# Keys and values from split fp32r operands, and part of a LayerNorm moved to GpSimd, in a gated cross-attention and expert layer

## The reference, cut to what matters

```python
xn = layernorm(x)
q = xn @ Wq + bq;  k = ctx @ Wk + bk;  v = ctx @ Wv + bv          # per head
attn = softmax(q k^T / 4);  a = attn @ v
x1 = x + tanh(g_xattn) * (concat(a) @ Wo + bo)
S  = sigmoid(layernorm(x1) @ Wg)                                  # routing
for each expert e:                                                # 896 tokens with the largest S
    h = gelu(layernorm(x1)[I_e] @ W1_e + b1_e)
    out[I_e] += tanh(g_ffn) * (h @ W2_e + b2_e) * S_e
```

## Time and profile before

| | |
|---|---|
| time, three runs | 893.86, 895.79 (median), 897.25 us |
| the profiled execution | 894.2 us, its span 892.4 us |
| PE busy over the span | 814.0 us (91%) |
| DVE busy | 708.3 us (79%) |
| ACT busy | 571.2 us (64%) |
| POOL busy | 286.0 us (32%) |
| mean granted TensorE clock | 0.961 of full |

### The profile page before, as it was taken

One profiled execution on the slowest core, in us unless ns is written; L12 is line 12 of the kernel. 1 busy time (PEld: TensorE's weight loads), 2 busy tenths in 40 slices (PEclk: granted clock), 3 DMA queues, 4 the chain that ended last, 5 costly groups with the idle time before them and its releaser, 6 DMA issues. The chain is left out here.

```text
span 892.4 us, 22315 instructions
## 1 busy us (share of the span) xinstructions
PE 814.0 (91%) x8336; PEld 667.8 (75%) x8336; DVE 708.3 (79%) x1900; ACT 571.2 (64%) x1251; POOL 286.0 (32%) x269
## 2 busy tenths in 40 slices
PE   5989999999999999999996118999999999999995
PEld 3555888888888888888775006989898988888885
DVE  6888999999999999999875784787676767764542
ACT  2655877787777777877664214847576675849470
POOL 4760111011111111110100603366465655644504
PEclk9999999999999999999998557999999999999998
DMA  7843666776676676666610304162525344453303
GB/s 190 196 93 89 153 157 153 169 180 155 151 184 152 157 165 165 173 154 150 160 33 29 106 1 134 44 153 50 135 54 136 58 130 102 97 131 67 38 6 41
DMA packets 96210, 104.62 MB, mean 117 GB/s; under 512 B 11744, under 2 KB 92272, under 8 KB 96112
## 3 DMA queue, kind: packets, MB, share of 16 engines
q1 hardware_dynamic: 84128, 88.50, 38.5%
q0 software_dynamic: 10752, 14.69, 9.6%
q10 hardware_dynamic: 1232, 0.12, 0.1%
HBM read 39.60 MB, written 14.68 MB: 61 GB/s over the span
## 5 line engine op out<-in xcount | busy, mean ns | idle before, releaser
L485 DVE TENSOR_REDUCE a_nm<-a_pS 112x1 f32<-112x375 f32 x342 | 177.3, 538 | 4.7 <-PE a_pS L791 4.1
L1772 PE MATMUL e_p<-w2hl,e_hh 128*128 128x512 f32 x440 | 156.9, 397 | 0.0
L725 POOL TENSOR_TENSOR a_kp<-a_k_rest,a_kp 128x375 bf16<-128x375 f32 x56 | 50.4, 900 | 323.7 <-ACT a_kp L326 323.7
L785 PEld LDWEIGHTS a_pT<-a_qst,a_kst 98*128 98x128 bf16 x1536 | 102.8, 99 | 40.8 <-issue 11.7
L785 PE MATMUL a_pT<-a_qst,a_kst 98*128 98x112 bf16 x1536 | 123.5, 212 | 1.7 <-ACT a_P L306 1.0
L1566 POOL DMA_INDIRECT out_dram<-e_y,e_idx x56 | 89.1, 1591 | 109.2 <-ACT e_y L1605 103.2
L1774 PE MATMUL e_p<-w2hl,e_hl 128*128 128x256 f32 x440 | 122.8, 279 | 0.0
L1652 DVE TENSOR_TENSOR e_hl<-e_hid,e_hh 128x384 fp32r<-128x384 f32 (+1 forms) x128 | 77.8, 623 | 47.3 <-ACT e_hh L1598 46.3
L306 ACT ACTIVATE a_room<-a_pT 128x448 f32<-128x448 f32 x192 | 96.7, 543 | 28.1 <-PE a_pT L785 27.8
L791 PE MATMUL a_pS<-a_kst,a_qst 96*112 96x375 bf16 x342 | 107.8, 334 | 3.4 <-DVE a_nm L485 3.0
L306 ACT ACTIVATE a_P<-a_pT 128x448 f32<-128x448 f32 x192 | 97.7, 546 | 9.4 <-PE a_pT L785 8.1
(11 more groups left out here) (247 smaller groups left out, 1688.9 us busy)
## 6 DMA issues: line engine op xcount, KB each, us to landing
a_kst<-a_kp SPq DMA_DIRECT2D x192, 192.0 KB, 3.6
w<-in_L_ffn_W_dram SPq DMA_DIRECT2D x16, 1024.0 KB, 6.8
a_qst<-a_qp SPq DMA_DIRECT2D x96, 112.0 KB, 3.0
a_craw<-in_ctx_dram SPq DMA_DIRECT2D x32, 128.0 KB
a_room<-in_x_dram SPq DMA_DIRECT2D x8, 448.0 KB, 6.6
a_xb<-in_x_dram SPq DMA_DIRECT2D x32, 112.0 KB, 3.4
out_dram<-a_x SPq DMA_DIRECT2D x32, 112.0 KB, 2.2
xn_scratch<-a_x SPq DMA_DIRECT2D x32, 112.0 KB, 2.2
```

The source lines that it names most:

```text
L485: dve.tensor_reduce(nm[:, h:h + 1], s_bank(b, h)[0:LQ, 0:LK], AXX, ALU.max, negate=True).then_inc(s_used, 1)
L785: last = pe.matmul(pT[u % 2][:, j * LQ:(j + 1) * LQ], kst[b % 4][:, h, c * 128:(c + 1) * 128], q_of(b, slice(None), h), start=True, stop=True)
L1772: pe.matmul(p2[g % 2][:], hh[:, f, rows], T.w2hl[r % 2][:, f].rearrange("p q d -> p (q d)"), start=(f == 0), stop=(f == 7), skip_group_che ...
```

## The change

1. **Keys and values.** From batch 5 on (`EARLY_C`), cT, wk and wv are split into a high fp32r part and an fp32r rest. Each fp32 matmul becomes three fp32r matmuls into the same bank (high x high, high x low, low x high), padded from 375 to 376 columns. The split of the weights (once) and of cT (`context_high`, `context_low`, once a batch) is done on POOL.
2. **x1 and its LayerNorm.** wo and bo are multiplied by tanh(g_xattn) once on POOL. bo is added to the reloaded x on POOL (`x_biased`), so that `added` alone makes x1 on DVE; `gated` is gone. DVE keeps the statistics and the mean and variance. POOL does the root (`pow` with -0.5, then two Newton rounds) and the scaling to x2 (`x2_of`).
3. **Places.** k_rest, O, cc[0], ccT, x1, x2 and x2T lie in tiles of the prologue that are free by then.
4. **Order.** `weighted(m)` comes near the start of step m instead of `weighted(m+1)` at the end of it; each exponential into a P buffer waits for the `weighted` quarter that read it. PE's, ACT's and DVE's lists are in a new order, and SP's: the row maxima and the queries go ahead of two thirds of the key DMAs, and `x_again(m+2)` takes the place of `x_again(m)`.

```diff
+        tail, xn_flat = room[:, 24 * LQ:], xnT[:].rearrange("p k n -> p (k n)")
+        k_rest = [tail[:, t * LK:(t + 1) * LK] for t in range(2)]
+        cTh, cTl = ([sb(f"cT{p}{i}", [128, LK2], F32R) for i in range(4)] for p in "hl")
...
@@ SP, main loop @@
                 if live(m + 4, 3):
                     stack_keys(m + 4, (0, 1))
-                    stack_keys(m + 4, (2, 3))
-                if live(m):
-                    x_again(m)
-                if live(m + 4, 3):
-                    stack_keys(m + 4, (4, 5))
                 if live(m + 2, 1):
                     row_max(m + 2)
                 if live(m + 5, 4):
                     stack_queries((m + 5) // 2, (3, 4, 5) if (m + 5) % 2 else (0, 1, 2))
+                if live(m + 4, 3):
+                    stack_keys(m + 4, (2, 3))
+                    stack_keys(m + 4, (4, 5))
+                if live(m + 2):
+                    x_again(m + 2)
@@ ACT @@
+                if c == 0:
+                    wait(act, o_ready, 4 * b + quad - 3)
                 act.activation(P[quad][:, c, :], pT[u % 2][:, 0:4 * LQ], ACT.Exp).then_inc(exp_done, 1)
@@ DVE @@
+                dve.wait_ge(xb_ready, b + 1)
                 dve.wait_ge(wo_ready, b + 1)
-                dve.tensor_tensor(xo[:], pM[0][0:LQ, 0:D], bo[:], ALU.add).then_inc(wo_read, 1)
-            def gated(b):
...
-                dve.scalar_tensor_tensor(xo[:], xo[:], gx[0:LQ], xb[p][:], ALU.mult, ALU.add).then_inc(x1_ready, 1)
+                dve.tensor_tensor(xo[:], pM[0][0:LQ, 0:D], xb[p][:], ALU.add).then_inc(x1_ready, 1)
@@ POOL @@
+            def x_biased(b):
+                pool.wait_ge(xb_loaded[b % 2], 16 * (b // 2 + 1))
+                pool.tensor_tensor(xb[b % 2][:], xb[b % 2][:], bo[:], ALU.add).then_inc(xb_ready, 1)
+            def root(b):
+                pool.wait_ge(mv_ready, b + 1)
+                pool.tensor_scalar(ve[:], mv[b % 2][:, 1:2], EPS, None, ALU.add).then_inc(root_set, 1)
+                pool.tensor_scalar(nvh[:], mv[b % 2][:, 1:2], EPS, -0.5, ALU.add, ALU.mult).then_inc(root_set, 1)
+                pool.tensor_tensor(y[:], ve[:], mhalf[:], ALU.pow).then_inc(root_set, 1)
+                for k in range(2):
+                    pool.tensor_scalar(yy[:], y[:], y[:], nvh[:], ALU.mult, ALU.mult).then_inc(root_set, 1)
+                    pool.tensor_scalar(y[:], yy[:], 1.5, y[:], ALU.add, ALU.mult).then_inc(root_set, 1)
+            def x2_of(b):
+                pool.tensor_scalar(x2[b % 2][:], x1[b % 2][:], mv[b % 2][:, 0:1], y[:], ALU.subtract, ALU.mult)\
+                    .then_inc(x2_ready, 1)
+            def context_high(b):
+                pool.wait_ge(ct_copied, b + 1)
+                pool.tensor_copy(cTh[b % 4][:, 0:LK], cT[b % 4][:]).then_inc(ct_high, 1)
+            def context_low(b):
+                pool.tensor_tensor(cTl[b % 4][:, 0:LK], cT[b % 4][:], cTh[b % 4][:, 0:LK].bitcast(F32), ALU.subtract).then_inc(ct_split, 1)
             for m in range(FIRST, LAST):
                 if live(m + 5, EARLY_K):
                     k_low_part(m + 5, 0)
+                if live(m + 6, EARLY_C):
+                    context_low(m + 6)
+                if live(m):
+                    root(m)
+                if live(m + 5, EARLY_K):
                     k_low_part(m + 5, 1)
+                if live(m):
+                    x2_of(m)
+                if live(m + 2):
+                    x_biased(m + 2)
+                if live(m + 7, EARLY_C):
+                    context_high(m + 7)
@@ PE @@
-                pe.matmul(k_bank(b, t)[:, 0:LK], wk[:, t, :], cT[b % 4][:], start=True, stop=True).then_inc(k_ready[t], 1)
+                pe.wait_ge(ct_split, b - EARLY_C + 1)
+                pe.matmul(out, wkh[:, t, :], cTh[b % 4][:], start=True, stop=False)
+                pe.matmul(out, wkh[:, t, :], cTl[b % 4][:], start=False, stop=False)
+                pe.matmul(out, wkl[:, t, :], cTh[b % 4][:], start=False, stop=True).then_inc(k_ready[t], 1)
...
+                    pe.matmul(out, cTh[b % 4][:, k0:k0 + n], wvh[:], start=True, stop=False)
+                    pe.matmul(out, cTh[b % 4][:, k0:k0 + n], wvl[:], start=False, stop=False)
+                    last = pe.matmul(out, cTl[b % 4][:, k0:k0 + n], wvh[:], start=False, stop=True)
```

More of the change, by code:

```diff
@@ new lines, in _ @@
+            pool.wait_ge(scaled, 3)
+            pool.wait_ge(wk_ready, 1)
+            pool.wait_ge(wq_ready, 2)
+            pool.wait_ge(wv_loaded, 16)
+            for t in range(2):
+                pool.wait_ge(q_ready[t], 3 * G)
+            for t in cTh + cTl:
+                pool.memset(t[:, LK:LK2].bitcast(F32), 0.0).then_inc(pads_zero, 1)
+            pool.tensor_copy(wkh[:], wk[:]).then_inc(w_high, 1)
+            pool.tensor_copy(wvh[:], wv[:]).then_inc(w_high, 1)
+            pool.wait_ge(w_high, 2)
@@ L958, in _ @@
                 if live(m + 2, 1):
+                    scores_s(m + 2, 10)
+                if live(m + 1):
+                    scores_t(m + 1, 1)
+                if live(m):
+                    bank_free(m, C_PIECES, "weighted")
+                    weighted(m, 0)
+                    weighted(m, 1)
+                    weighted(m, 2)
+                    weighted(m, 3)
+                if live(m + 2, 1):
+                    scores_s(m + 2, 11)
+                if live(m + 1):
+                    scores_t(m + 1, 2)
+                if live(m + 2, 1):
                     scores_s(m + 2, 12)
                 if live(m + 1):
-                    scores_t(m + 1, 1)
+                    scores_t(m + 1, 3)
                 if live(m + 2, 1):
                     scores_s(m + 2, 13)
+                if live(m):
+                    o_transposes(m, m)
+                if live(m + 1):
+                    scores_t(m + 1, 4)
+                if live(m + 2, 1):
+                    scores_s(m + 2, 14)
                 if live(m - 2):
@@ L966, in _ @@
                 if live(m + 1):
-                    scores_t(m + 1, 2)
+                    scores_t(m + 1, 5)
                 if live(m + 2, 1):
-                    scores_s(m + 2, 14)
+                    scores_s(m + 2, 15)
                 if live(m + 5, EARLY_K):
@@ L972, in _ @@
                 if live(m + 1):
-                    scores_t(m + 1, 3)
-                if live(m + 2, 1):
-                    scores_s(m + 2, 15)
-                if live(m + 1):
-                    scores_t(m + 1, 4)
+                    scores_t(m + 1, 6)
                 if live(m + 3, 2):
@@ L981, in _ @@
                     scores_s(m + 3, 0)
-                if live(m):
-                    o_transposes(m, m)
                 if live(m + 2, 1):
@@ L986, in _ @@
                     values(m + 2, 0)
-                if live(m + 1):
-                    scores_t(m + 1, 5)
-                    scores_t(m + 1, 6)
                 if live(m + 3, 2):
                     scores_s(m + 3, 1)
-                    scores_s(m + 3, 2)
                 if live(m + 2, 1):
@@ L995, in _ @@
                     values(m + 2, 1)
+                if live(m + 1):
+                    scores_t(m + 1, 7)
+                    scores_t(m + 1, 8)
+                if live(m + 3, 2):
+                    scores_s(m + 3, 2)
                 if live(m + 5, EARLY_K):
                     keys_at_once(m, m + 5, 1)
-                if live(m + 1):
-                    scores_t(m + 1, 7)
                 if live(m + 3, 2):
@@ L1019, in _ @@
                     ct_transposes(m + 6)
+                if live(m - 1):
+                    x2_transposes(m, m - 1)
+                if live(m + 1):
+                    scores_t(m + 1, 10)
+                if live(m + 3, 2):
+                    scores_s(m + 3, 6)
+                if live(m + 1):
+                    scores_t(m + 1, 11)
                 if live(m + 3, 2):
                     scores_s(m + 3, 7)
-                if live(m + 3, 1):
-                    scores_s(m + 3, 8)
                 if live(m):
@@ L1026, in _ @@
                 if live(m + 3, 1):
+                    scores_s(m + 3, 8)
                     scores_s(m + 3, 9)
[L1028 to L1038 removed]
 class Tiles:
```

202 lines of the change are left out of this document (90 added, 112 removed).

## The result

The changed kernel takes 886.82 us (median of 4 runs, 883.57 to 890.51) against 896.26 us for the kernel before in the same comparison. The ratio is 0.990, 95% interval 0.9856 to 0.9944. The forecast was faster, at 876. It is faster, by 9.4 us where some 20 were forecast. The measured time lies inside the stated range and outside the forecast's own range of 871 to 882: the sign was right, the size was half.

What follows compares the result with a forecast made beforehand. PE and DVE were taken to bound the 12.70 us step nearly equally. 12.2 + 4.8 + 3.5 - 0.9 = 19.6 off 894.2 gives 874.6, and 1.6 more for the median 876.2; range 869 to 890, own range 871 to 882.

Steps and rivals of the forecast that it cites:

- What bounded the kernel before: Main loop: PE (about 12.35 us) and DVE (about 12.46) bound the 12.70 us step; relieving one brings about 0.2.
- Keys and values, 0.45 us a step: PE in the main loop: fp32r matmuls save 0.22 on keys and 0.23 on values a batch, 12.2 us in all.
- DVE: Main loop: 1.8 to 2.9 us of work leaves DVE, which keeps 9.6 to 10.7 us a step.
- The second load of x: Main loop: DVE's 6.4 us of waits for this load go, worth 3.5 us of time, bounds 2 and 5.
- POOL: Main loop: 7.2 us of POOL work a step, root 2.0 of it, with 2.8 and 3.0 us of slack.
- The rival of a late POOL: Root before x2: if over 5.0 us, x2 is late for PE, each further us adding 28; chance 0.08.
- POOL and DVE blocking each other: Rival: SBUF instructions wait for each other, 2.5 us a step returns to DVE, time about 891; chance 0.08.
- The new order on PE: Main loop: PE's list might run without a gap; half of 0.35 us a step, 4.8 us gained; step 12.1.
- The rival of the row maxima: Their DMA takes 3.1 to 3.4 us instead of 2.3 and ends the step; time 882 to 891; chance 0.13.
- SP: DMA issue: row maxima land in time; four key DMAs end 5.4 us into the next step, needed at 6.2.
- The ends: Last batch's root and scaling lie open on the path: 0.9 us lost, bounds 0 and 3.
- 4.8 gaps: Main loop on PE: half of the 0.35 us of stretched places a step, 0.17 x 28, bounds 0 and 9.8.

Runs made afterwards that it cites:

- e5: e1 plus five unused bn_stats among the maxima of each step on DVE; 882.4 us, ratio 0.986 to the kernel before.
- e1: Changed kernel with key DMAs (2, 3) issued ahead of the row maxima and (4, 5) right behind, ahead of the queries; 874.8 us, ratio 0.978 to before.
- e3: e1 with EARLY_C = 32, so all keys and values are single fp32 products and no context is split; 883.4 us, ratio 0.9875 to before.
- e7: Kernel before with only the second load of x issued earlier, x_again(m + 1) at the end of SP's step; 889.0 us, ratio 0.994 to before.
- e8: Changed kernel with the three query DMAs moved behind the last key DMAs, nothing moved ahead of the row maxima; 873.0 us, ratio 0.976 to before.
- e6: e1 plus two unused tensor_scalar of 112 x 192 on GpSimd ahead of x2_of in each step; 880.7 us, ratio 0.984 to before.
- e2: Changed kernel with EARLY_C = 32, so all keys and values are single fp32 products and no context is split; 897.4 us, ratio 1.002 to before.
- e4: Changed kernel with key DMAs (4, 5) issued later, behind context(m + 8); 907.1 us, ratio 1.010 to before.

## Why the prediction was half right, by its own steps

**What bounded the kernel before: right.** Two engines nearly full. e5 takes DVE's relief out of e1, e3 takes the cheaper products out, and either gives a step of 12.5 to 12.6; only both together give 12.1 to 12.2. Measured from e7's 12.68, in which the wait for x is gone already, one relief brings 0.1 to 0.2 (the prediction said about 0.2) and both bring 0.6 (e8).

**Keys and values, 0.45 us a step: right** in the shortest steps, and not shown whole as 12.2 us: e3 against e1 gives 8.6. In the changed kernel's own trace:

```profile
304.00 0.33 PE L865 MATMUL a_pO<-a_cTl,a_wkh 128*128 128x376 f32 x1
304.17 0.33 PE L866 MATMUL a_pO<-a_cTh,a_wkl 128*128 128x376 f32 x1
304.34 0.37 PE L810 MATMUL a_pT<-a_qst,a_kst 98*128 98x112 bf16 x4
...
305.29 0.28 PE L937 MATMUL a_pM<-a_wvh,a_cTh 128*128 128x256 f32 x1
305.40 0.28 PE L938 MATMUL a_pM<-a_wvl,a_cTh 128*128 128x256 f32 x1
305.52 0.28 PE L939 MATMUL a_pM<-a_wvh,a_cTl 128*128 128x256 f32 x1
```

0.17 and 0.12 us from start to start, as in the earlier trace rows, fresh weights and all.

**DVE: right** (10.38 busy, with its idle time under `weighted`). **The second load of x: a little too small,** 3.5 where e7 gives 4.0 in the 27 steps that the term was read from, and 5.5 in the whole time (3.5 to 7.3 by its interval); I had bounds of 2 and 5.

**POOL: right in sum, and its slack held.** `pow` had no row; it is short, and the small dependent instructions are somewhat longer than I took:

```profile
L706 POOL TENSOR_SCALAR a_yy<-a_y,a_nvh 112x1 f32<-112x1 f32 x47 | 16.0, 341 | 5.0
L703 POOL TENSOR_TENSOR a_y<-a_ve,a_mhalf 112x1 f32<-112x1 f32 x23 | 13.2, 573 | 1.8
L708 POOL TENSOR_SCALAR a_y<-a_yy,a_y 112x1 f32<-112x1 f32 x48 | 12.7, 265 | 5.0
```

The root takes 2.8 us (forecast 2.0), x2 is ready 7.6 us into the step (forecast 6.9) and is asked for at 10.2. e6 spends 2.1 of the remaining 2.6 without a longer step. The rival of a late POOL is refuted for the loop.

**POOL and DVE blocking each other: there, and harmless.** `max_low` (L505) takes 294 ns here, against 109 before:

```profile
L505 DVE TENSOR_TENSOR a_mm<-a_nm,a_mm 112x16 bf16<-112x16 f32 x24 | 7.1, 294 | 0.8
```

Some 0.2 us a step, in front of slack, as the rival's own working said. The reductions from PSUM keep their 540 ns (537 before) with POOL busy four times as long; the rule of the Trainium skill ("SBUF — State Buffer", "SBUF: two separate sides") that the prediction cited (only VectorE instructions with two SBUF inputs or in a two-port mode meet the lock) agrees with both rows.

**The new order on PE: right as a layout.** The shortest steps are 12.02 to 12.07, and e8's mean is 12.09, for a forecast of 12.1. T2, o_transposes and wo wait for nothing in 150:450 and x2_transposes for 1.0 us in all, as worked out. The rival of the row maxima isn't seen in the changed kernel; it appears with e1's order alone (2.0 to 7.0 us in 150:450 of e1, e3, e5 and e6), when four key DMAs are put in front of it.

**SP: the step that failed.** The prediction said: "Four key DMAs now end near 17.4, 5.4 in the next step, against S0 at 6.2." I worked with the best issue time, 2.5 us for four, and the median landing, 3.5 us, and took 0.8 us of margin for enough. Measured were 6.7 instead of 5.4 in the step shown, where the four issues took the 2.5 us: the landing was the part that failed, 4.7 us for the last DMA instead of 3.5. The median landing is even a little lower than before, but the last DMA of such a burst doesn't get the median:

```profile
L214 SPq DMA_DIRECT2D a_kst<-a_kp x138: 546/598/1951, 151.8 to 435.7; - x138
...
DMA to landing us min/median/max: 2.6/3.2/5.1
```

In 15 of the 22 bursts of four key DMAs in 150:450 the issues take 2.5 to 2.7 us, and the last DMA lands 4.2 to 5.1 us after its own issue. In the kernel before, where the queries don't stand right in front of such a burst, this is 3.4 to 4.6, in e1 3.2 to 4.0. In the other seven bursts one issue takes 1.1 to 1.95 us where 0.6 is usual, but then the last DMA lands within 3.0 to 3.5. From the first issue to the last landing these seven take 5.7 to 6.6 us and the 15 take 6.1 to 7.0. So a slow issue inside the burst is not what makes the keys late. The change has put eight issues (row maxima, queries, keys) in a row where they are late. Its price is 12.62 - 12.09 = 0.53 us a step, 14 us in 27 steps, the same 0.53 that PE's weight loads wait for the key DMAs. A second fault lies behind it: I listed the late keys in the sum with their margin, and gave them no place among the rivals and no chance, although a late POOL, with three times the margin, had one. Nor did its list of what would show it wrong name a wait of S0.

**The ends.** Forecast 0.9 lost. PE's wait for the last x2 grew from 2.73 to 4.07 us, and from the last copy of O to the last x2_transposes it is 10.88 instead of 10.17 us, 0.7 more:

```profile
482.04 0.61 PE L909 MATMUL a_pM<-ident,a_wq_raw 112*128 112x112 f32 x2 [4.07 <-POOL a_wq_raw L712]
```

In this execution the last store of x2 then landed late as well and held the next stage 1.8 us (SP waited 3.4 us for it against 1.6 before). e1's shorter end (14.23 us from the last copy to routing, against 15.45) says that this part was chance; e1's is 1.2 more than the 12.99 before, near the forecast. The step before the last copy took 10.25 us in this execution, three of them at a granted clock of 0.50, against 8.90 in e1 and e8 at 1.00; the forecast had no term for the clock.

**The balance.** Forecast per profiled execution 19.6 us: 12.2 products, 4.8 gaps, 3.5 x, less 0.9. e8, the changed kernel with the one fault in SP's order mended, has 21.5 by the medians, 20.0 of them in the 27 steps. Of these 4.0 are x's by e7, which leaves 16.0 for products and gaps together (forecast 17.0). The changed kernel is 10.6 us above the forecast of 876.2. The late keys cost it some 14, so e8 lies 3 below the forecast: the terms were sound, and somewhat low in sum.

## What to carry to other kernels

When two engines are freed in one edit, the next bound may be the engine that computes nothing: lay out the queue that issues the DMAs with the same care as the others, and with its bad case (the last landing of a burst), not with medians. A margin that is smaller than the spread of the thing it is for is a rival, with a price. A wait on a DMA whose issue depends on this step's work is a loop: only work outside the loop hides under it (e2, as far as it shows). And a wait that grows can cost more than itself: in e4 the granted clock fell behind the longest waits.

## What was not expected of the hardware

A DMA issue on SP takes 0.4 to 0.6 us as a rule and now and then 1.2 to 1.95 (598 ns median and 1951 at most for the key DMAs), about once a step where I followed SP through a step; what it waits for isn't settled. The last of four key DMAs lands 4.2 to 5.1 us after its issue behind row maxima and queries, and 3.2 to 4.0 where it goes out ahead of them (e1). The order of issues at equal traffic moved the kernel by 13.8 us (886.8 to 873.0). A `pow` of a 112 x 1 operand on GpSimd takes 0.57 us, about twice its neighbours.
